# Transformer block on one core: a part of each side group moved between two softmax blocks, and the order of VectorE's steps changed

## What is computed

```python
mod = (_silu(c) @ wmod).reshape(4, 6, 1, -1)          # shifts, scales and gates of each batch
h = _layernorm(x) * (1 + ca) + sa
qkv = (h @ Wqkv.T + bqkv).reshape(B, 16, S, 3 * hd)    # 16 heads of width 8, one head = 64 rows of x
scores = einsum('bhsd,bhtd->bhst', q, k) / sqrt(hd)    # 1024 x 1024 for each batch and head
vals = einsum('bhst,bhtd->bhsd', softmax(scores), v).reshape(B, S, D)
x = x + ga * (vals @ Wo.T + bo)
h = _layernorm(x) * (1 + cb) + sb
probs = softmax(h @ router_w.T)                        # 8 experts, the two largest are kept
out = ((combined_top2(h @ expert_weights) + remap_bias) * topk_w).sum(0)
x = x + gb * out
```

## Time and profile before

| | |
|---|---|
| median of 3 runs | 594.01 us (593.64 to 594.24) |
| profiled execution | 592.45 us, of which the span is 590.7 us |
| busy: TensorE (PE), ScalarE (ACT), VectorE (DVE), GpSimd (POOL) | 92%, 83%, 58%, 37% of the span |
| granted TensorE clock | full, apart from the last 5% of the span, where it is 0.6 |
| 512 exponents L522 | 482.6 us busy, 1030 ns each |

### The profile page before, as it was taken

How to read it: one execution, slowest core, us unless ns; L and a number is a source line. 1 busy time by engine, 2 the same in 40 slices (tenths; PEclk the granted TensorE clock), 3 DMA queues, 4 the chain that set the end, 5 groups by cost and what they waited for, 6 DMA issues and landing times.

```text
span 590.7 us, 14331 instructions
## 1 busy us (share of the span) xinstructions
PE 542.7 (92%) x4046; PEld 202.0 (34%) x4046; DVE 341.5 (58%) x1276; ACT 487.3 (83%) x546; POOL 219.3 (37%) x436
## 2 busy tenths in 40 slices
PE   7499999999999999999999999999999999999944
PEld 5233323333333333333333333333333323333222
DVE  4325566656566666656565656556656666554564
ACT  1389998989888989998989899898989898989700
POOL 1103333333344432343444433333444333433347
PEclk9999999999999999999999999999999999999966
DMA  4383333333233333332233333332333332322000
GB/s 96 96 221 80 80 92 93 84 90 86 70 79 87 85 89 85 90 79 72 72 87 87 85 85 91 83 75 69 85 87 83 85 94 71 85 72 78 22 18 13
DMA packets 85496, 48.43 MB, mean 82 GB/s; under 512 B 61508, under 2 KB 76240, under 8 KB 85456
## 3 DMA queue, kind: packets, MB, share of 16 engines
q1 hardware_dynamic: 84400, 47.43, 31.9%
q10 hardware_dynamic: 1056, 0.46, 0.4%
HBM read 32.91 MB, written 14.94 MB: 81 GB/s over the span
## 4 chain that ended last, share of the span: by engine, by line
PE 59%; ACT 18%; DVE 9%; issue 7%; SPq 2%; POOL 2%; DVEq 2%; DMA 1%; POOLq 0%; ACTq 0%
PE ps_attn L673 20%; ACT probs L522 18%; PE ps_scores L655 16%; PE ps_side L703 9%; PE ps_side L590 4%; DVE sums_inv L980 2%; PE ps_side L597 2%; DVE attn L974 1%; PE ps_side L686 1%; DVE weighted L1060 1%; PE ps_side L584 1%; PE ps_side L682 1%; DVEq L949 1%; PE ps_side L606 1%; PE ps_side L690 1%
## 5 line engine op out<-in xcount | busy, mean ns | idle before, releaser
L522 ACT ACTIVATE probs<-ps_scores 128x1024 f32<-128x1024 f32 x512 | 482.6, 1030 | 68.4 <-PE ps_scores L655 66.2
L673 PE MATMUL ps_attn<-probs,values 128*32 128x512 f32 x2048 | 273.8, 607 | 2.9 <-DVE attn L974 2.9
L655 PE MATMUL ps_scores<-query_stack,key_stack 32*128 32x512 f32 x1024 | 133.5, 500 | 17.7 <-ACT probs L522 4.1
L655 PEld LDWEIGHTS ps_scores<-query_stack,key_stack 32*128 32x128 f32 x1024 | 51.7, 183 | 172.1 <-ACT probs L522 139.8
L411 POOL TENSOR_SCALAR var_eps<-moments 128x1 f32<-128x1 f32 x64 | 12.3, 193 | 247.4 <-DVE moments L991 222.2
L703 PE MATMUL ps_side<-experts_gated,h2T 128*128 (+2 forms) x228 | 75.6, 413 | 0.0
L673 PEld LDWEIGHTS ps_attn<-probs,values 128*32 128x32 f32 x2048 | 40.6, 108 | 67.6 <-issue 57.0
L913 DVE TENSOR_TENSOR qkT<-ps_side,bqk_cols 128x256 f32<-128x256 f32 x32 | 13.6, 425 | 58.8 <-PE ps_side L703 46.5
L1060 DVE TENSOR_TENSOR weighted<-ps_side,coef 128x128 f32<-128x128 f32 (+1 forms) x114 | 46.5, 407 | 1.4 <-PE ps_side L703 1.4
L974 DVE COPY attn<-ps_attn 128x512 f32<-128x512 f32 x32 | 22.1, 691 | 38.3 <-PE ps_attn L673 37.6
L936 DVE TENSOR_REDUCE norm_max<-ps_side 128x1 fp32r<-128x32 f32 x31 | 5.9, 191 | 63.7 <-PE ps_side L703 61.1
(11 more groups left out here) (119 smaller groups left out, 503.0 us busy)
## 6 DMA issues: line engine op xcount, KB each, us to landing
key_stack<-k_scr SPq DMA_DIRECT2D x128, 128.0 KB, 2.7
query_stack<-q_scr SPq DMA_DIRECT2D x124, 64.0 KB, 2.3
q_scr<-qk_parts SPq DMA_DIRECT2D x186, 32.0 KB, 2.0
k_scr<-qk_parts SPq DMA_DIRECT2D x64, 64.0 KB, 1.7
a_scr<-attn SPq DMA_DIRECT2D x128, 18.0 KB
sums<-a_scr SPq DMA_DIRECT2D x32, 64.0 KB, 2.1
attnT<-a_scr SPq DMA_DIRECT2D x32, 64.0 KB, 2.3
out_dram<-out_all SPq DMA_DIRECT2D x32, 64.0 KB, 1.7
```

Of the source, the lines that this page charges most:

```text
L522: nc.scalar.activation(probs[:, k % RING, g, :], ps_scores[:, slot(parity, k, g), :], ACT.Exp, scale=SCALE)\
L655: mm = nc.tensor.matmul(out_, key_stack[p0:p0 + 32, parity, 2 * k:2 * k + 2, :].rearrange("p j r -> p (j r)"), query_stack[p0:p0 + 32, par ...
L673: mm = nc.tensor.matmul(ps_attn[q:q + 32, :], values[:, parity, g, k, :], probs[:, k % RING, g, h * HALF:(h + 1) * HALF], start=(k == 0), ...
```

## The change

Four things change. Every piece has two experts. The first expert of a piece (`half` 0) goes into the pair of blocks, behind the weighted sum of the even block, by a new function `ahead`, with the waits of the `drained` function in front of it; the second (`half` 1) stays in the side group. The value projection moves from side2 to side1, with `a_values` from stage 2 to stage 1, into other columns of the bank. On VectorE the moments of the second norm (`c_moments`) come behind the weighing and `a_bounded` in stage 0, and `c_vals` moves from the end of stage 3 to the end of stage 2.

```diff
-    PIECES = ((0, 1), (1, 3), (3, 5), (5, 8))
+    PIECES = ((0, 2), (2, 4), (4, 6), (6, 8))
...
-            def a_project_v(u1, ring):
+            def a_project_v(u1, ring, col):
...
-            def c_experts(ps, y, b, ring, piece):
+            def c_experts(ps, y, b, ring, piece, half=None):
...
                 e0, e1 = PIECES[piece]
+                last = e1
+                if half == 0:
+                    e1 = e0 + 1
+                if half == 1:
+                    e0 = e0 + 1
...
-                nc.tensor.matmul(ps[:, 4 * P - (e1 - e0) * D:4 * P], h2T[:, ring, :], rhs, start=True, stop=True)\
-                    .then_inc(experts_done[piece], 1)
+                mm = nc.tensor.matmul(ps[:, 4 * P - (last - e0) * D:4 * P - (last - e1) * D], h2T[:, ring, :], rhs, start=True, stop=True)
+                if e1 == last:
+                    mm.then_inc(experts_done[piece], 1)
...
                 if past < 2 <= before:
                     c_transpose(ps, at[-1])
+                if before >= 2 and after >= 1:
+                    a_project_v(at[2], 1 - parity, P)
                 if past < 4 <= before:
-                    c_experts(ps, at[-4], batch[4], parity, 3)
+                    c_experts(ps, at[-4], batch[4], parity, 3, None if after < 0 else 1)
...
                 if past < 2 <= before:
                     reached(pe, ev["h2T_done"], at[-1])
+                if before >= 2 and after >= 1:
+                    reached(pe, ev["values_done"], at[2])
...
+            def ahead(at, batch, parity, before, after, side):
+
+                if side == 0 and before >= 4:
+                    drained3(at, before, after, 0)
+                    c_experts(ps_side, at[-4], batch[4], parity, 2, 0)
+                if side == 1 and before >= 4:
+                    drained0(at, before, after, 0)
+                    c_experts(ps_side, at[-4], batch[4], parity, 3, 0)
+                if side == 2 and before >= 3:
+                    drained1(at, before, after, 0)
+                    c_experts(ps_side, at[-3], batch[3], 1 - parity, 0, 0)
+                if side == 3 and before >= 3:
+                    drained2(at, before, after, 0)
+                    c_experts(ps_side, at[-3], batch[3], 1 - parity, 1, 0)
...
                     elif before:
                         weigh(at[-1], at[0], 1 - parity, KT - 2 + k)
+                    if k == k0:
+                        ahead(at, batch, parity, before, after, k0 // 2)
...
                 v.tensor_tensor(x1[:, ring, :], ps[:, 0:P], x_gated[:], ALU.add).then_inc(ev["x1_done"], 1)
+
+            def c_moments(y1, ring):
                 reached(dve, ev["x1_done"], y1)
...
                 if after >= 1:
                     a_bounded(banks[0][0:1, P:2 * P], at[2], 1 - parity)
+                if past < 2 <= before:
+                    c_moments(at[-1], parity)
...
                     c_weigh(banks[1], at[-3], parity, 3)
+                if before >= 2 and after >= 1:
+                    a_values(at[2], 1 - parity, P)
...
                 if after >= 2:
                     a_qk_parts(at[2], at[3])
+                if after >= 0 and before:
+                    c_vals(t)
...
-                if past < 1 <= before:
+                if after < 0 and past < 1:
                     c_vals(t)
```

More of the change, by code:

```diff
@@ L591, in a_project_qk @@
                 mm.then_inc(ev["qk_ps_done"], 1)
[L593 removed]
+            def a_project_v(u1, ring, col):
                 for n in range(G):
                     for odd in range(2):
[L597 removed]
+                        mm = nc.tensor.matmul(ps_side[odd * R:(odd + 1) * R, col + n * R:col + (n + 1) * R],
                                               hT[:, ring, n * R:(n + 1) * R], wvT[:, odd].rearrange("p k d -> p (k d)"),
@@ L724, in side0 @@
                 if past < 4 <= before:
-                    c_experts(ps, at[-4], batch[4], parity, 2)
+                    c_experts(ps, at[-4], batch[4], parity, 2, None if after < 0 else 1)
             def drained0(at, before, after, past):
@@ L753, in side2 @@
                     a_project_qk(at[3], parity)
-                if after >= 1:
-                    a_project_v(at[2], 1 - parity)
+                if before < 2:
+                    a_project_v(at[2], 1 - parity, 2 * P)
                 if past < 3 <= before:
-                    c_experts(ps, at[-3], batch[3], 1 - parity, 0)
+                    c_experts(ps, at[-3], batch[3], 1 - parity, 0, None if after < 0 else 1)
             def drained2(at, before, after, past):
@@ L776, in side3 @@
                 if past < 3 <= before:
-                    c_experts(ps, at[-3], batch[3], 1 - parity, 1)
+                    c_experts(ps, at[-3], batch[3], 1 - parity, 1, None if after < 0 else 1)
             def counts(t, before):
@@ L783, in counts, with two_blocks @@
                 return at, batch
-            def two_blocks(at, parity, before, k0, exact):
+            def ahead(at, batch, parity, before, after, side):
[11 more added lines that the diff above has]
+                    c_experts(ps_side, at[-3], batch[3], 1 - parity, 1, 0)
+            def two_blocks(at, batch, parity, before, after, k0, exact):
                 for k in (k0, k0 + 1):
@@ L821, in tile @@
                             pe.wait_ge(setup_dve, SETUP_GATES + before)
-                        drained1(at, before, after, 0)
+                        if before < 3:
+                            drained1(at, before, after, 0)
                         side2(ps_side, at, batch, parity, before, after, 0)
                     if k0 == 6:
-                        drained2(at, before, after, 0)
+                        if before < 3:
+                            drained2(at, before, after, 0)
                         side3(ps_side, at, batch, parity, before, after, 0)
@@ L1069, in written0, with written1 @@
                     reached(dve, ev["normT_done"], at[2])
-            def written1(at, before, past):
+            def written1(at, before, after, past):
                 if past < 4 <= before:
                     reached(dve, experts_done[3], at[-3])
+                elif before >= 2 and after >= 1:
+                    reached(dve, ev["v_ps_done"], at[2])
             def written2(at, before, after, past):
@@ L1079, in written2 @@
                     reached(dve, experts_done[0], at[-2])
-                elif after >= 1:
+                elif before < 2:
                     reached(dve, ev["v_ps_done"], at[2])
+                elif after >= 2:
+                    reached(dve, ev["qk_ps_done"], at[3])
             def written3(at, before, after, past):
@@ L1124, in tile @@
                     c_router_top(at[-2])
-                written1(at, before, past)
+                written1(at, before, after, past)
                 if before == 0:
@@ L1142, in tile @@
                     a_qk(at[3])
-                if after >= 1:
-                    a_values(at[2], 1 - parity)
+                if before < 2:
+                    a_values(at[2], 1 - parity, 2 * P)
                 if past < 3 <= before:
```

18 lines of the change are left out of this document (10 added, 8 removed).

## The result

The kernel before took 594.12 us in the runs beside it (median of four, 593.64 to 596.58), the changed one 610.13 (median of four, 609.0 to 615.19): a ratio of 1.0277, 95% interval 1.0214 to 1.0341. It is slower, 3.1 us beyond the predicted 607.0 and inside the predicted range of 597 to 617. The profiled execution of the changed kernel took 610.22 us with a span of 608.4; before it was 592.45 and 590.7, faster than any of the timed runs of that kernel. The granted clock averages 0.976 in the changed one and 0.980 in the one before.

What follows compares the result with a forecast made beforehand. It took the order in which TensorE and ScalarE release each other as the bound. Terms 7.0 - 0.2 + 1.4 + 4.2 + 0.6 = +13.0 on the profiled 592.45 give 605.4, with 1.56 for the median 607.0; range 597 to 617.

Steps and rivals of the forecast that it cites:

- Product ahead, 0.42: Each one-expert product behind a pair's first weighted sum costs 0.42 and fills a 0.19 wait: +0.23 a pair.
- The rival in which loads hide under the sum: Products ahead hide weight loads under the weighted sum and cost 0.17, so the kernel gets faster, 581; chance 0.07.
- Sides: Side groups change by shorter products (-0.16, -0.32, none, -0.19) and the value projection (+0.38 at k0 = 2, -0.38 at k0 = 4).
- k0 = 4, wait for the values, 0.15 (0 to 0.3): TensorE's wait before the k0 = 4 product ahead: values ready 1.58 into the pair against 1.43; 28 x 0.15 = 4.2.
- The chain of the moments: VectorE's later moments end 1.7 into the k0 = 2 pair, normalised rows start at 2.9, eventually making the values late.
- k0 = 0, last weighing, 0.05: Wait before the k0 = 0 product ahead: weighing ready at 1.42 against 1.43; taken as 0.05 (0 to 0.15), 28 x 0.05 = 1.4.
- k0 = 2 and 6, no wait: Waits before these products ahead end about 1.0 and under 1.0 into the pair, so cost nothing.
- Loop-back: Where the loop turns back, 12 tiles: -0.21 from earlier c_vals, +0.19 from side3 time not recovered; net -0.2.
- The 0.19 that the sequencer was said to hold back: At the loop's turn TensorE's sequencer can't follow the shorter side3, so 0.19 is not recovered (between 0 and 0.22).
- The cover of 0.6: Earlier c_vals costs nothing: reciprocal and product are done by 307.7, 0.6 before side3 ends at 308.29.
- ScalarE's idle time: Predicted sign of the mechanism: ScalarE's idle time goes up by the whole difference.
- the tail: In the last tiles piece 2's weighing stands between sum and moments in two drained tiles: +0.6, between 0 and 1.

Runs made afterwards that it cites:

- e4: Changed kernel; before the k0 = 4 product ahead, the values' wait comes last and the gated-experts wait stays only in written-out tiles; 608.33 us, ratio 1.0209.
- e8: Changed kernel with the second norm's moments back in front of the weighing of piece 2; 617.28 us, ratio 1.0367.
- e2: Kernel before with only the first expert of pieces 1, 2 and 3 put ahead, VectorE's order and value projection as before; 609.45 us, ratio 1.0251.
- e3: Kernel before with only c_vals moved in front of stage 3; 592.66 us, ratio 0.9957.
- e5: Kernel before with c_vals in front of stage 3 only in the loop's tiles 4 to 27; 592.22 us, ratio 0.9961.
- e6: Kernel before with c_vals early in the loop only, plus the router's logits put behind the first sum at k0 = 6; 590.18 us, ratio 0.9924.
- e9: Kernel before with c_vals early in the loop, plus logits and the next rows' transpose behind the first sum at k0 = 6; 593.32 us, ratio 0.9977.
- e10: Kernel before with c_vals early in the loop, plus whole expert piece 0 behind the first sum at k0 = 4; 589.63 us, ratio 0.992.
- e7: Changed kernel with c_vals early only in the loop; 607.81 us, ratio 1.022.
- e1: Changed kernel with expert products whole in the side groups again and their waits in front of the side; 596.05 us, ratio 1.0023.

## Why the prediction was right, and where it was off

- **Product ahead, 0.42.** Measured 0.41 to 0.42 at k0 = 0, 2, 4 and 6; the distance from sum to second scores is 1.41, as said. The rival in which loads hide under the sum fell: behind eight weighted matmuls a product of two costs as much as behind other products, and its first weight load starts at 316.14, 0.01 before its first matmul, after 0.84 without a load. That rival would have followed from the rule in the Trainium skill (TensorE: Matmul & The Clock Gate, "Step-by-step: what each phase is for") that the next weights load while a matmul runs; no product ahead in these traces does.
- **Sides.** Right for side0 and side3; the errors of the other two have opposite signs. Side2 is 0.865 long rather than 1.06: its product, counted at 0.42, costs 0.32 behind the projection's 128-column matmuls (314.72 - 314.40); the other 0.10 is not traced. Side1 is 0.10 longer than counted: its transpose costs 0.26 (309.25 - 308.99), and 0.16 in the kernel before (315.52 - 315.36).
- **k0 = 4, wait for the values, 0.15 (0 to 0.3).** Mis-sized, and by the wrong cause: 0.33 (distances 1.51 and 1.16 instead of 1.00). The chain of the moments came out as worked out (they end 1.64 into the k0 = 2 pair, the normalised rows start at 2.76, where 1.7 and 2.9 had been said), but the experts' input starts 310.51 - 310.05 = 0.46 into the next pair rather than 0.59, and the values were done 1.39 into it rather than 1.53. The array is free at 1.44, so VectorE is in time. What was missing is the sequencer's work behind the values, 0.545 in even and 0.20 in odd tiles, where the prediction had counted 0.05 for the semaphore; it had named the address and further waits only in its upper end of 0.3. Even tiles pay more because there three instructions stand behind the wait for the values. e4 took 0.2 of the even tiles' part away. e8 moved the chain of the moments and changed nothing here.
- **k0 = 0, last weighing, 0.05.** It is nothing in even tiles (1.01) and 0.18 in odd ones: 0.09 on average, inside its bounds. In odd tiles the weighing ends 1.36 into the pair, as worked out (1.37), and the product follows 0.25 behind that, not 0.05: the same missing term.
- **k0 = 2 and 6, no wait.** Right; e2 and e8 show that at k0 = 2 this hangs on the norm standing in front of the moments.
- **Loop-back.** The -0.21 by c_vals is shown by e3 and e5. The 0.19 that the sequencer was said to hold back was about 0.10: the k0 = 6 pair is 4.31 long with the turn behind it and 4.21 elsewhere.
- **The start, 3.7 us, was not in the prediction.** It let products ride from tile 4 on and counted nothing before. At the turn from tile 2 to tile 3 the read of the attention is issued 15.1 us behind the start of tile 2 (72.86 - 57.75), where it is 12.3 in tile 16 (313.92 - 301.63), and c_vals now stands in front of work that could have run:

```profile
76.47 0.95 DVE L1010 RECIPROCAL sums_inv<-sums 128x128 f32<-128x128 f32 x1 [5.51 <-DMA attnT<-a_scr]
...
78.56 0.80 PE L682 MATMUL ps_side<-wo_gated,valsT 128*128 128x128 f32 x2 [2.50 <-DVE logits L1043]
```

VectorE waits 5.5 us for the read, with the norm maximum, `hT` and the logits behind it in its order, and TensorE then stands still for 2.5. The cover of 0.6 worked out for the loop said nothing of this tile. The kernel before has a smaller stop in the same place:

```profile
75.64 0.95 DVE L980 RECIPROCAL sums_inv<-sums 128x128 f32<-128x128 f32 x1 [1.84 <-DMA attnT<-a_scr]
...
77.06 0.46 PE L682 MATMUL ps_side<-wo_gated,valsT 128*128 128x128 f32 x2 [0.60 <-DVE valsT L982]
```

This read landed 3.6 us after its issue in the changed kernel and 2.2 after it in the kernel before. How much of the 3.7 the change causes is open. e5, e6, e9 and e10 have the same code up to tile 4 as the kernel before; they start that tile 1.9 later, 0.5 earlier, and 0.2 and 0.8 later. By the start of tile 5 all of the other profiles, these four too, are 1.5 to 6.2 us behind the kernel before's (106.88; the nearest, e9, 108.41; the changed kernel 111.79). So the one profile of the kernel before probably had a quick start, and a part of the 3.7 is that. The medians point the same way: they differ by 16.0 and the two profiles by 17.8. The early c_vals (e7, 1.3) may be another part; e3 and e5 show next to nothing of it.
- **ScalarE's idle time** was to rise by the whole difference. By the page it rises from 590.7 - 487.3 = 103.4 to 608.4 - 493.6 = 114.8, by 11.4 of 17.7; the rest is that its busy time grew, since fewer exponents overlap their neighbour (350 of them instead of 389).

Added up: 12.4 predicted for the products, waits and c_vals and 0.6 for the tail, 13.0; measured 14.0 from tile 4 to the end, and 3.7 ahead of it. That the medians differ by 3.1 from the forecast and not by 4.7 comes from the changed kernel's profiled execution lying at its median, where 1.56 had been added. The mechanism, a product's fixed part paid four times more against a gap of 0.19, was forecast rightly and is what e1 shows. That the sum a tile comes so near (0.45 against 0.44) is luck in part: a wait put too low by 0.18 stands against a side counted too long by 0.20.

## What to carry to other kernels

Splitting a product to fill a gap pays the fixed part of a product again; compare that part (0.25 here) with the gap (0.19) before the columns. Moving a whole step into the gap keeps the price, and is worth at most the gap. A wait that moves forward in a queue takes its sequencer work along, and what it waits for must be early by that much too (0.2 to 0.55 here); of several waits, the one that ends last should stand last. Edits that come in a bundle are worth timing alone: here the reciprocal's move gains 0.4% by itself, inside a change that loses 2.8%.

## What the runs showed of the hardware that was not expected

In the changed kernel a stall is followed by a slow stretch. The window from 79 to 86 us, one row for the kernel before, the changed one and e5 (window, us, busy time and count of PE, PEld, DVE, ACT, POOL, granted clock, DMA share, GB/s):

```profile
79.00:86.00 7.00, 6.74 (x63) 2.51 (x55) 3.99 (x23) 6.53 (x8) 3.14 (x8) 1.00 0.45 117
```

```profile
79.00:86.00 7.00, 7.00 (x44) 2.09 (x47) 4.08 (x21) 4.08 (x5) 1.90 (x5) 0.59 0.42 115
```

```profile
79.00:86.00 7.00, 6.88 (x45) 1.33 (x37) 4.30 (x23) 5.89 (x7) 3.14 (x8) 0.76 0.42 112
```

In the changed kernel TensorE had stood still for 2.5 us in front of this window. A weighted sum of eight matmuls then took 1.94 (from 80.12), where it takes 1.06 in the loop: the lower level of 1.2 GHz. A mean of 0.59 says that most of the window ran at it. The idle time costs a second time. In e5 TensorE had stood still for 1.37 us, and the window's clock is 0.76. It doesn't follow every such stall: behind 1.74 us in e2 and 1.63 in e10 the same window has 1.00. The kernel before had 0.60 of standing still and 1.00.

Work of a sequencer stands in no row of a timeline; it shows there as "issue" (0.45 in the k0 = 4 pair) or is put down to the releaser (e2, e8), though 0.40 lies behind the releaser's end. From the end of the releasing VectorE step to the product it took 0.20 with one sequencer instruction behind that wait and 0.545 with three (tiles 6 to 27 of the changed kernel). Taking one wait away and putting another ahead of the late one brought 0.2 back in even tiles.

A small product behind a weighted sum is dear: the logits with their 8 columns cost 0.14 inside a side (318.31 - 318.17 in the changed kernel), and behind a weighted sum 0.24 with a transpose after them (e9) and 0.32 with the scores after them (e6).

```profile
318.17 0.29 PE L690 MATMUL ps_side<-routerT,h2T 128*128 128x8 f32 x2
318.31 0.37 PE L606 MATMUL ps_side<-head_sum,squares 128*128 128x16 f32 x2
```
